# Four of sixteen VectorE copies of transposed probabilities moved to ScalarE in a differential-attention and expert-attention kernel

## The reference, cut to what matters

```python
# layer 1: differential attention, H = 8 heads, D = 32, two softmaxes per head
q = (x @ Wq) -> (B, 2H, T, D) * D**-0.5;  k, v = split(x @ Wkv)
attn_w = softmax(q k^T)                         # (B, 2H, T, T), T = 1024
attn_w = attn_w[:, :, 0] - lam * attn_w[:, :, 1]
attn = attn_w @ v                               # v is (B, H, T, 64)
attn = gamma * attn / (rms(attn) + 1e-8) * (1 - LAMBDA_INIT)
x = x + attn @ Wout
...
```

## Time and profile before

| | |
|---|---|
| median of 3 runs | 1553.21 us (1552.88 to 1555.73) |
| profiled execution, its own time | 1555.85 us |
| its span, first to last instruction | 1554.1 us |
| mean granted TensorE clock | 0.973 of full speed |
| head stage with all engines at work | about 60 to 1118 us of the span |
| busy over the span: TensorE, VectorE, ScalarE, GpSimd | 85%, 82%, 68%, 71% |

### The profile page before, as it was taken

One profiled execution on the slowest core, in us unless ns is written; L12 is line 12 of the kernel. 1 busy time (PEld: TensorE's weight loads), 2 busy tenths in 40 slices (PEclk: granted clock), 3 DMA queues, 4 the chain that ended last, 5 costly groups with the idle time before them and its releaser, 6 DMA issues. The chain is left out here.

```text
span 1554.1 us, 27938 instructions
## 1 busy us (share of the span) xinstructions
PE 1314.9 (85%) x8882; PEld 803.2 (52%) x8882; DVE 1280.1 (82%) x2129; ACT 1049.4 (68%) x1967; POOL 1107.2 (71%) x715
## 2 busy tenths in 40 slices
PE   2888888888888888888888888888853899999997
PEld 1444444444444444444444444444432899899997
DVE  5899999899999999998999999998866566656665
ACT  2887777777777777777777777787633455445553
POOL 3898888888888888888888888888834333323330
PEclk8899999999999999999999999999975999999999
DMA  4221111111111112111111211110030000000000
GB/s 110 72 74 46 46 28 50 42 52 31 46 46 27 46 37 57 34 46 46 27 46 34 57 37 46 28 28 1 1 54 1 5 6 8 8 8 7 8 9 10
DMA packets 51461, 52.99 MB, mean 34 GB/s; under 512 B 17057, under 2 KB 32929, under 8 KB 51361
## 3 DMA queue, kind: packets, MB, share of 16 engines
q1 hardware_dynamic: 51360, 51.76, 13.2%
HBM read 7.68 MB, written 2.10 MB: 6 GB/s over the span
## 5 line engine op out<-in xcount | busy, mean ns | idle before, releaser
L1214 DVE TENSOR_REDUCE negmax<-score_ps 128x1 f32<-128x1024 f32 x512 | 618.8, 1216 | 87.9 <-PE score_ps L569 86.0
L904 ACT ACTIVATE prob<-score_ps,negmax 128x1024 f32<-128x1024 f32 x512 | 571.5, 1116 | 129.4 <-DVE negmax L1214 117.7
L465 POOL TENSOR_TENSOR prob<-prob 128x1024 f32<-128x1024 f32 x256 | 604.2, 2360 | 21.3
L569 PE MATMUL score_ps<-ka,qa 128*128 128x512 f16 x1024 | 313.0, 388 | 119.4 <-ACT prob L904 105.9
L463 POOL TENSOR_SCALAR prob<-prob,ccol 128x1024 f32<-128x1024 f32 x256 | 287.2, 1122 | 104.7 <-DVE ccol L1227 104.2
L592 PE MATMUL trans_ps<-ident,prob 128*128 128x128 f32 x2048 | 283.9, 277 | 7.4 <-POOL prob L465 3.0
L592 PEld LDWEIGHTS trans_ps<-ident,prob 128*128 128x128 f32 x2048 | 240.3, 142 | 75.8 <-DVE probT L318 17.7
L598 PE MATMUL attn_ps<-probT,v_sb 128*64 128x512 f32 x1024 | 276.7, 620 | 1.1 <-DVE probT L318 1.1
L517 POOL TENSOR_TENSOR xs<-xnT,rw_all 128x2048 f32 (+1 forms) x32 | 115.5, 3612 | 210.9 <-PE t_ps L722 204.1
L569 PEld LDWEIGHTS score_ps<-ka,qa 128*128 128x128 f16 x1024 | 72.4, 98 | 277.5 <-ACT prob L904 233.4
L318 DVE COPY probT<-trans_ps 128x512 f32<-128x512 f32 x256 | 174.0, 680 | 2.4 <-PE trans_ps L592 2.4
(11 more groups left out here) (195 smaller groups left out, 1423.6 us busy)
## 6 DMA issues: line engine op xcount, KB each, us to landing
qa<-split SPq DMA_DIRECT2D x256, 64.0 KB, 2.0
ka<-split SPq DMA_DIRECT2D x256, 64.0 KB, 2.0
xg<-xnT SPq DMA_DIRECT2D x16, 512.0 KB, 3.0
resid<-in_L_attn_x SPq DMA_DIRECT2D x4, 512.0 KB, 6.0
wg<-in_L_attn_Wkv SPq DMA_DIRECT2D x32, 64.0 KB, 1.9
out<-yo SPq DMA_DIRECT2D x32, 64.0 KB, 1.5
wg<-in_L_attn_Wq SPq DMA_DIRECT2D x16, 64.0 KB, 1.9
ew<-in_L_ffn_q_proj SPq DMA_DIRECT2D x1, 512.0 KB, 4.5
```

Source lines behind the costliest of these rows:

```text
L465: pool.tensor_tensor(prob1[:, u, :], prob1[:, u, :], prob2[:, u, :], ALU.add).then_inc(mix_ok, 1)
L569: mm = pe.matmul(score_ps[:, sub, kh * HALF:(kh + 1) * HALF], qa[:, par, head * 2 + sub, q0:q0 + P], ka[:, par, head * 2 + sub, kh * HALF: ...
L904: act.activation(prob2[:, s % 4, :] if sub else prob1[:, s % 4, :], score_ps[:, sub, :], ACT.Exp, bias=negmax[:, s % 2, sub:sub + 1], accu ...
L1214: dve.tensor_reduce(negmax[:, s % 2, sub:sub + 1], score_ps[:, sub, :], AX.X, ALU.max, negate=True).then_inc(max_ok, 1)
```

## The change

In slots 6, 7, 14 and 15 of every 16, ScalarE copies bank 1 of `trans_ps` to `probT`, behind its exp of `sub` 1 and ahead of the copies of that slot's fill; VectorE doesn't. In the other twelve slots nothing changes. No wait or semaphore is another: the copy waits for `trans_ok` and raises `probT_ok[1]` from whichever engine makes it.

```diff
+ACT_COPIES = (6, 7, 14, 15)
...
                     copy_probT(act, act_copy, s, n, it, 0, first, last)
                     if s < SLOTS:
                         softmax(1)
+                    if s % UNITS in ACT_COPIES:
+                        copy_probT(act, act_copy, s, n, it, 1, first, last)
...
                         row_max(n + 1, s + 1, 0)
-                    copy_probT(dve, dve.tensor_copy, s, n, it, 1, first, last)
+                    if s % UNITS not in ACT_COPIES:
+                        copy_probT(dve, dve.tensor_copy, s, n, it, 1, first, last)
```

## The result

The changed kernel takes 1520.39 us (median of 4 runs, 1517.87 to 1521.09) against 1553.28 in the same comparison: a ratio of 0.9782, 95% interval 0.9765 to 0.9799. Its profiled execution took 1520.76 us, with a span of 1519.0. 1517 was forecast, within 1510 to 1545.

A forecast was written before the change was run, and what follows sets the result against it. Bound: ScalarE's exp (8, 1) waiting 1.84 us behind attn_n, held by GpSimd's add. Gains of 31.0, 4.0 and 1 make 36.0 us; 1555.85 - 36.0 = 1519.9, less 2.6 to the median: 1517, range 1510 to 1545.

The forecast's parts named there:

- Rival 1: Slot 7: GpSimd's add goes before attn_n, whose end stays; nothing won, 1553 us, chance 0.14 (missed in part: 1535, 0.08).
- the lead of 0.10 us: Slot 7: attn_n would start at 607.84, 0.10 us ahead of GpSimd's add at 607.94, and so go first.
- Rival 2: attn_n and GpSimd's add only slow each other; attn_n ends 0.60 us earlier, 14 us won: 1539 us, chance 0.06.
- What GpSimd's add pays: Slot 7: with attn_n first, GpSimd's add takes 0.30 us more, against 1.14 us of idle time behind it.
- Rival 3: Slot 6: ScalarE's copy delays exp (7, 0) by up to 0.25 us and the add goes first: 1560 us, chance 0.08.
- the doubt: Slot 7: if attn_n really starts only at 607.92, its lead over the add is 0.02 us and the race is open.
- the usual halves: 22 halves like the one shown: slot 8 falls from 5.41 to 4.00 us, 1.41 us each, 31.0 us together.
- The two in the last iteration: Halves with no projection behind them and waits up to 2.75 us: between 1.41 and 2.32 each, 2.0 taken, 4.0 together.
- The first iteration: Slots 6, 7, 14 and 15 have no attn_n, but VectorE is nearly full: 0 to 2.4 us, 1 taken.
- the five halves behind a jump back: ScalarE itself comes 2.1 us late there and hides VectorE's lateness: no gain.
- 1519.9: Time for an execution like the profiled one: 1555.85 - 36.0 us; that one was 2.6 us over the median of 1553.21.

The follow-up runs named there:

- the instruction with one tensor beside the add: Kernel before, with attn_n replaced by a VectorE sum of the same 512 elements (one SBUF input), leaving out the normalisation: 1521.38 us, ratio 0.9772.
- the order alone: Kernel before, no copy moved to ScalarE; in slots with attn_n, VectorE makes attn_n first and the bank 1 copy behind it: 1524.50 us, ratio 0.9794.
- the two pairs: Changed kernel with ScalarE's copies only in slots 7 and 15 (1520.35 us, ratio 0.9761), or only in 6 and 14 (1555.86 us, ratio 0.9996).

## Why the prediction was right

**The cause.** An instruction with two SBUF tensors is held while GpSimd runs one: right, by the instruction with one tensor beside the add. The change acts through the order, not the load: right, by the order alone and by the two pairs. Rival 1 (the gap is missed) is what two small instructions more would have brought; the lead of 0.10 us that it was weighed by was real, and the true margin is wider than the records' starts show by more than 0.02 and less than 0.07 us, since `attn_n` still wins when it starts 0.02 us behind the add and loses at 0.07. Rival 2 (plain contention) is out: all or nothing was measured. What GpSimd's add pays was put too low: 0.43 us (2.79 against 2.36), not 0.30, for here `attn_n` starts just as the scaling ends (492.70 against 492.71), and there it had started 0.55 us ahead of that. The idle time of 1.14 us behind the add is gone: the next scaling follows at once. Rival 3 (ScalarE's queue) named a cost that isn't there in slot 6 (1.59 against 1.58 us) but is there in slots 9 and 10, where nothing hides it.

I had leaned on the Trainium skill, VectorE: DVE Perf Modes, The DRAIN you can't avoid, for the doubt that VectorE's next instruction may start only when the last has ended; the same section adds that one that isn't held starts earlier. The doubt can be weighed now: even at a recorded start 0.02 us behind the add's, with the reciprocal ahead of it recorded until 0.08 us later still, `attn_n` went first. Whether its true start is later than the recorded one, no run shows; the race isn't lost by it.

**The sum, by starts of `attn_n` in both traces.** 22 x 1.41 = 31.0 us was forecast for the usual halves. Such a half went from 33.96 to 32.53 us in most cases, and 22 of them gave 31.9. The two in the last iteration gave 3.4 and 3.2 us (from 35.10 and 33.79 to 31.68 and 30.64), against 2.0 each and a bound of 2.32. What I had not looked at is TensorE's clock, the last but two of the numbers in a row by windows. In the kernel before it falls behind the wait of 2.75 us in each of these two halves; in the changed kernel it stays at 1.00. With the copies moved in slots 1, 2, 9 and 10, `attn_n` is held just as long (2.42 us) and exp waits 2.76 us, but the clock stays up:

```profile
1057.00:1061.00 4.00, 4.00 (x15) 1.92 (x13) 2.83 (x6) 2.85 (x7) 3.92 (x3) 0.57 0.02 4
```
```profile
1070.00:1074.00 4.00, 3.89 (x25) 2.25 (x24) 3.17 (x7) 4.00 (x8) 3.92 (x3) 1.00 0.02 4
```

(The first is of the kernel before, the second of that other one.) There the two halves take 34.09 and 32.94 us. So about 1 us of each gain is the clock's, and the 2.4 and 2.3 that are left lie at the bound. The first iteration gave 0.5, not 1. And the five halves behind a jump back, which I had put at nothing, became 3.6 us longer in all (35.77 us on average, against 35.05). That is the clock again, and the last section has the rows; by itself the moved `attn_n` is worth nothing there, as forecast, for at full clock such a half takes 34.70 us before the change and 34.71 with copies in slots 7 and 15. 31.9 + 6.6 + 0.5 - 3.6, less 0.2 in the tail, is the 35.1 us by which the span fell; 36.0 was forecast. Two terms were off, one each way and mostly by what the clock did, and made up for one another: that the sum is so close is in part luck.

**From the sum to the median.** 1519.9 was worked out for an execution like the profiled one, and the profiled one took 1520.76. I then took off 2.6 us, because the profiled execution of before was so much over its median. That was chance: in the experiments the medians of before lie around 1555.85, and the profiled execution after is 0.4 us from its median. This is most of the 3.4 us by which 1517 is too low.

## What to carry to other kernels

An instruction that is long on average may be short and held. Compare its end with the ends on the engine that it could share something with, before taking its duration for work; if it always ends the same time behind the other's end, a new place in the order can be worth more than any relief. In this kernel a VectorE instruction with two SBUF tensors belongs into the moment when GpSimd waits for itself, and a gain that hangs on a lead of 0.1 us should be made safe by the order, or by a form with one SBUF tensor. Before a copy is moved to another engine, ask what is next on that engine and whether it is already free to go. And before two kernels are compared half by half, read the granted clock of each half.

## What was not expected of the hardware

**The race is won or lost within 0.06 us.** By recorded starts VectorE still goes first at 0.02 us behind GpSimd's add, and is held at 0.07. If VectorE has lost, it waits for the end of GpSimd's instruction, nearly all of 2.36 us. GpSimd, where it comes second, only pays 0.43 to 0.50 us (2.79 and 2.86 against 2.36). VectorE's turn comes even where GpSimd goes from one instruction straight into the next, as with L1242 at 490.75 us.

**TensorE's clock behind a jump back.** Where iterations 1 to 6 begin anew, ScalarE is 2.1 us late and TensorE has nothing to do for 2.66 us, before the change (574.9 to 577.6 us) and after. In the changed kernel the clock then falls to its lower level. The first three rows are of that kernel, the last is of the one with copies in slots 7 and 15 only, behind one of its jumps:

```profile
426.50:429.00 2.50, 0.03 (x1) 0.03 (x2) 0.80 (x2) 1.28 (x3) 2.42 (x3) 1.00 0.12 30
429.00:431.00 2.00, 2.00 (x7) 0.51 (x8) 1.38 (x2) 1.50 (x3) 1.92 (x1) 0.80 0.42 98
431.00:434.00 3.00, 3.00 (x15) 2.45 (x15) 2.00 (x4) 2.06 (x4) 1.89 (x2) 0.56 0.47 109
```
```profile
562.00:565.00 3.00, 2.31 (x12) 0.95 (x13) 1.67 (x2) 2.29 (x6) 2.59 (x2) 1.00 0.43 100
```

A full clock reads 1.00 here, 2.4 GHz, and 1.2 GHz is 0.50; windows of 1 us behind this jump reach 0.50. The four transposes of the fill start at 430.77 and take 1.12 us, against 0.66 at full clock behind the jump at 576.33 in the kernel before, where all windows read 1.00 behind the same idle time.

| kernel | halves behind a jump with a lowered clock | with a full clock |
|---|---|---|
| before | 1: 36.40 us | 4: 34.70 to 34.72 us |
| changed | 5: 35.67 to 35.90 us | none |
| copies in slots 7 and 15 | 4: 36.18 to 37.06 us | 1: 34.71 us |
| changed, with one small instruction | 4: 35.71 to 36.46 us | 1: 34.71 us |

So the long halves are those with a lowered clock, within one kernel too. Why it falls behind one jump and not behind the next stays open: ScalarE's idle time doesn't tell them apart, with 2.06 us ahead of a fall in the changed kernel and 2.06 us ahead of none in the one before.
